# A state-space block and two attention layers on one core: token shift by transfers, packed step products, another set-up order, GpSimd's rotary work widened, the denominators' inverse on VectorE

## The reference, cut to what matters

```python
# state-space block, x: (16, 256, 128)
u = silu(causal_conv4(x @ in_w + in_b))
delta = softplus((u @ dt1_w + dt1_b) @ dt2_w + dt2_b)      # rank 16 between
h_t = exp(delta*A) * h_(t-1) + (exp(delta*A) - 1)/A * B * u     # 16 states per channel
y = (sum_n C_n h_n + D*u) * silu(x @ gate_w + gate_b)
x = layernorm(x + y @ out_w + out_b)
# twice:
h = shift_token(x)              # second 64 features come from the token before
q, k, v = split(h @ wqkv)       # 8 heads of 64
q, k = rotary_xpos(l2norm(q)*qs, l2norm(k)*ks)
x = x + local_attention(q, k, v, window 64, one window back) @ wo
h = layernorm(shift_token(x)) * g + b
a, g = split(h @ w1 + b1);  x = x + (a * gelu(g)) @ w2 + b2
# and a last residual and layernorm
```

## Time and profile before

| what | value |
|---|---|
| median of 3 runs | 1104.92 us (1102.85 to 1107.98) |
| the profiled execution's own time | 1106.03 us |
| its span in the profile | 1103.8 us |
| mean granted TensorE clock | 0.967 |
| instructions | 27452 |

### The profile page before, as it was taken

One profiled execution on the slowest core, in us unless ns is written; L12 is line 12 of the kernel. 1 busy time (PEld: TensorE's weight loads), 2 busy tenths in 40 slices (PEclk: granted clock), 3 DMA queues, 4 the chain that ended last, 5 costly groups with the idle time before them and its releaser, 6 DMA issues.

```text
span 1103.8 us, 27452 instructions
## 1 busy us (share of the span) xinstructions
PE 967.1 (88%) x10784; PEld 593.9 (54%) x10784; DVE 863.2 (78%) x1184; ACT 832.3 (75%) x1909; POOL 671.5 (61%) x513
## 2 busy tenths in 40 slices
PE   4677779799999899999999999998999999996775
PEld 1222345456555465557465646465665766665463
DVE  7776897898888877998799878996988875642543
ACT  4455777886998669886988699877879887783570
POOL 2004764688578666876567857685656777661561
PEclk9988899899999999999999999999999999998897
DMA  6000100000000100000000110010001011010010
GB/s 217 10 15 1 26 1 15 14 18 15 16 16 17 39 20 16 21 16 19 22 17 16 35 26 15 12 40 10 21 7 30 16 25 26 7 25 6 14 32 10
DMA packets 22354, 25.59 MB, mean 23 GB/s; under 512 B 2710, under 2 KB 14545, under 8 KB 22225
## 3 DMA queue, kind: packets, MB, share of 16 engines
q1 hardware_dynamic: 20783, 22.49, 7.9%
q10 hardware_dynamic: 1442, 1.34, 0.4%
HBM read 9.13 MB, written 2.10 MB: 10 GB/s over the span
## 4 chain that ended last, share of the span: by engine, by line
PE 47%; ACT 18%; issue 13%; DVE 11%; POOL 11%; ACTq 1%; POOLq 0%; DVEq 0%
PE M L1257 11%; PE YY L1257 10%; ACT prob L926 8%; PE AA L1257 8%; PE C L1257 6%; DVE scan L1073 4%; PE BB L1257 4%; POOL rn L761 4%; PE BB L1407 2%; PE BB L1395 2%; POOL rden L767 2%; PE C L1458 1%; ACT qkT L914 1%; ACT probT L895 1%; POOL kr L780 1%
## 5 line engine op out<-in xcount | busy, mean ns | idle before, releaser
L1073 DVE TENSOR_TENSOR_SCAN scan<-du,decay 128x1028 f32<-128x1028 f32 (+1 forms) x160 | 297.4, 1898 | 8.7 <-PE YY L1257 4.9
L926 ACT ACTIVATE prob<-BB,nbias,rn 128x128 f32<-128x128 f32 x472 | 208.7, 464 | 48.0 <-POOL nbias L774 47.3
L761 POOL TENSOR_TENSOR rn<-ssc,expo 128x16 f32<-128x16 f32 x64 | 212.5, 3321 | 19.8 <-ACT prob L926 15.1
L871 ACT ACTIVATE decay<-delta,negA 128x1024 f32<-128x1024 f32 (+1 forms) x160 | 153.3, 985 | 16.6 <-DVE scan L1073 12.1
L767 POOL TENSOR_TENSOR rden<-den,minus 128x8 f32<-128x8 f32 x64 | 126.5, 1976 | 49.5 <-ACT prob L926 49.5
L1257 PE MATMUL YY<-scan,diag 64*64 64x512 f32 (+1 forms) x1280 | 142.7, 538 | 15.3 <-DVE scan L1073 15.2
L1257 PE MATMUL AA<-wqkv,hT 128*128 128x512 f32 x256 | 131.4, 638 | 11.8 <-DVE qks L1148 10.2
L756 POOL TENSOR_SCALAR ssc<-ss 128x16 f32<-128x16 f32 x64 | 47.7, 745 | 91.1 <-DVE ss L1130 90.2
L1130 DVE TENSOR_REDUCE ss<-sq 128x16 f32<-128x1024 f32 x64 | 77.3, 1208 | 29.4 <-ACT sq L889 29.3
L926 ACT ACTIVATION_READ_ACCUMULATOR prob<-BB,nbias,rn 128x1 f32 x472 | 99.8, 211 | 0.0
L1162 DVE TENSOR_REDUCE nmax<-BB 128x8 f32<-128x1024 f32 x59 | 71.9, 1218 | 31.8 <-PE BB L1257 31.6
(11 more groups left out here) (158 smaller groups left out, 2062.4 us busy)
## 6 DMA issues: line engine op xcount, KB each, us to landing
v_even<-v_odd SPq DMA_DIRECT2D x96, 128.0 KB, 2.3
x<-in_x SPq DMA_DIRECT2D x6, 256.0 KB, 3.8
wqkv<-in_wqkv SPq DMA_DIRECT2D x1, 1536.0 KB
xT<-in_xT SPq DMA_DIRECT2D x6, 256.0 KB, 3.8
out<-outb SPq DMA_DIRECT2D x6, 256.0 KB, 2.6
w<-in_w SPq DMA_DIRECT2D x1, 682.0 KB
xT<-in_xT SPq DMA_DIRECT2D x4, 128.0 KB, 2.6
x<-in_x SPq DMA_DIRECT2D x4, 128.0 KB, 4.4
```

Of the source, the lines that this page charges most:

```text
L761: pool.tensor_tensor(rn[:, q % 2, :], ssc[:, :], expo[:, 0:2 * HEADS], ALU.pow).then_inc(rn_sb, 1)
L871: act.activation(decay[:, at % A_RING, both(g), 1:], delta[:, both(g), :], ACT.Exp, scale=negA[:, n:n + 1]).then_inc(decay_sb, 1)
L926: ins = act.activation(prob[:, h, :], bank_of(q, a)[:, c * P:(c + 1) * P], ACT.Exp, bias=nbias[:, q % 2, h:h + 1], scale=rn[:, q % 2, h:h ...
L1073: dve.tensor_tensor_scan(state, step, a, 0.0, ALU.add, ALU.mult).then_inc(scan_sb, 1)
```

## The change

- **Shift.** `shift` moves from PE to SP. Three transfers copy x2 to a new buffer `xs`: the second 64 features one partition down, the row that crosses a tile boundary, and the first 64 features unchanged. `ffn_stats`, `ffn_norm` and GpSimd's `residual` use `xs` or wait for the transfers. The shift and carry matrices are gone, and M is no longer held.
- **Step products.** dt1_w is padded to 32 columns. `rank` makes four products 128x32, one per channel half and half of the tokens, on four groups of 32 partitions of one bank; `step_in` makes four products 64x128, each over half the tokens and one half of the rows, and the sum over channel halves falls to that product. ScalarE reads each result in one instruction.
- **Set-up.** ScalarE issues two transfers, loads the exponential's table, makes A and loads silu's table; the others move to SP. GpSimd clears three buffers. VectorE computes the coefficients before the convolution. Masks and rotation tables become steps of the order, behind group 0's scans. In group 0, ScalarE makes the gate before u.
- **Rotary sums and norms.** `rotate` adds cosine and sine products for q and k together, in place, and multiplies both with their norms. `qk_T` transposes the result in 16 and not 24 transposes. Softmax needs no scale, its bias is the row maximum itself, and `exp_bias` is gone.
- **Inverse.** `inverse` moves from POOL's power to VectorE's `reciprocal`, a step of DVE's order that waits for the tile's softmax.
- The written orders of all engines are new.

```diff
-                pool.tensor_tensor(kr[:, :], qkc[:, q % 2, 1, :], qks[:, q % 2, 1, :], ALU.add).then_inc(rope_add, 1)
+                both_qk = qkc[:, q % 2].rearrange("p a x -> p (a x)")
+                pool.tensor_tensor(both_qk, both_qk, qks[:, q % 2].rearrange("p a x -> p (a x)"), ALU.add).then_inc(rope_add, 1)
...
+                pool.tensor_tensor(all_heads, all_heads, rn[:, q % 2, :].unsqueeze(2).to_broadcast((P, 2 * HEADS, DH)),
                                    ALU.mult).then_inc(qk_sb, 1)
...
-                pool.tensor_tensor(rden[:, q % 2, :], den[:, q % 2, :], minus[:, :], ALU.pow).then_inc(rden_sb, 1)
+            def inverse(q):
+                dve.wait_ge(prob_sb, 2 * q + 2)
+                if q >= 2:
+                    dve.wait_ge(o_sb, q - 1)
+                dve.reciprocal(rden[:, q % 2, :], den[:, q % 2, :]).then_inc(rden_sb, 1)
...
-                act.wait_ge(nmax_sb, q + 1)
+                act.wait_ge(max_sb, q + 1)
...
-                                             bias=nbias[:, q % 2, h:h + 1], scale=rn[:, q % 2, h:h + 1],
+                                             bias=nmax[:, q % 2, h:h + 1],
...
+            def shift(f):
+                n, mid = tiles_of(QUAD[f][1]), D // 2
+                sp.wait_ge(x2_sb, f + 1)
+                if f:
+                    sp.wait_ge(hn_sb, f)
+                else:
+                    sp.wait_ge(zeros_late, 1)
+                sp.dma_start(xs[1:P, 0:n, mid:], x2[0:P - 1, 0:n, mid:]).then_inc(sh_in, 16)
+                sp.dma_start(xs[0:1, 1:n:2, mid:], x2[P - 1:P, 0:n:2, mid:]).then_inc(sh_in, 16)
+                sp.dma_start(xs[:, 0:n, 0:mid], x2[:, 0:n, 0:mid]).then_inc(sh_in, 16)
...
-                pe.wait_ge(rope_mul, 2 * q + 2)
-                for part in range(2):
+                pe.wait_ge(qk_sb, q + 1)
+                for a in range(2):
                     for c in range(PAIRS):
                         for w in range(2):
...
+                            ins = pe.transpose(bank_of(q, w)[:, (a * PAIRS + c) * WIN:(a * PAIRS + c + 1) * WIN],
+                                               qkc[half(w), q % 2, a, c * P:(c + 1) * P], ident[half(w), half(w)])
...
-                for h in range(HALF):
-                    ins = mm(Y[0][0:RANK, 0:tok_of(g)], dt1_w[:, h, :], u[:, ab(g, h), 1:], h == 0, h == HALF - 1)
+                for k in range(2):
+                    for h in range(HALF):
+                        lo = (2 * k + h) * PART
...
+                        mm(Y[0][lo:lo + PART, 0:n], dt1_w[:, h, :], rhs).then_inc(d1_ps, 1)
...
-                    mm(bk(Y[h], g), dt2_w[:, h * P:(h + 1) * P], bk(dt1_s, g)).then_inc(z_ps, 1)
+                    for k in range(2):
+                        mm(Y[k][:, h * n:(h + 1) * n], dt2_w[half(k), h * P:(h + 1) * P], dt1_s[half(k), 0:n]).then_inc(z_ps, 1)
```

The set-up's code, in the same cut:

```diff
             load_xT(0)
+            sp.dma_start(pv[:, :], t["pv"]).then_inc(w_cols, 16)
             sp.dma_start(gate_w[:, :], t["gate_w"]).then_inc(w_gate, 16)
+            sp.dma_start(dt1_w[:, :, :], t["dt1_w"].rearrange("(h p) r -> p h r", h=HALF)).then_inc(w_step, 16)
+            sp.dma_start(dt2_w[:, :], t["dt2_w"]).then_inc(w_step, 16)
...
+            act.dma_start(in_w[:, :], t["in_w"]).then_inc(w_first, 16)
+            act.dma_start(bv[:, 0:NST], t["bv"][0:NST].partition_broadcast(P)).then_inc(w_rates, 16)
+            load_table(EXP_AND_LN)
+            act.wait_ge(w_rates, 16)
+            act.activation(negA[:, :], bv[:, BV["A_log"]:BV["A_log"] + NST], ACT.Exp).then_inc(a_exp, 1)
+            load_table(SILU)
...
+            coefficients()
+            dve.wait_ge(w_cols, 16)
             convolve(0, 0)
             convolve(0, 1)
-            coefficients()
-            masks()
-            rotation_tables()
+            state_weights()
```

More of the change, by code:

```diff
@@ L96 @@
[L96 to L125, removed]
@@ L171 @@
-shift 18, probs_T 62, weighted 62, norm_T 18, out_T 62, probs_T 63, up_gate 18, weighted 63, up_a 18 0,
-up_a 18 1, up_a 18 2, out_T 63, down 18, attn_out 19, shift 19, norm_T 19, up_gate 19, up_a 19 0, up_a 19 1,
-up_a 19 2, down 19"""
+state_y 1 14, state_y 1 15, mamba_out 1, u_in 2, gate_in 2, rank 2, qk_in 1, step_in 2, layer_T 0 1, qk_T 0,
+qk_in 2, scores 0, v_in 2, skip 2, qk_in 3, qk_T 1, state_y 2 0, probs_T 0, weighted 0, scores 1, out_T 0,
+v_in 3, state_y 2 1, state_y 2 2, probs_T 1, qk_T 2, scores 2, weighted 1, state_y 2 3, state_y 2 4, state_y 2 5,
@@ new lines @@
+norm_T 1, out_T 4, probs_T 5, v_in 7, qk_T 6, up_gate 1, state_y 3 2, scores 6, state_y 3 3, qk_in 8, up_a 1 0,
+state_y 3 4, weighted 5, up_a 1 1, state_y 3 5, probs_T 6, up_a 1 2, out_T 5, qk_in 9, v_in 8, qk_T 7,
+weighted 6, scores 7, state_y 3 6, state_y 3 7, out_T 6, state_y 3 8, down 1, probs_T 7, v_in 9, qk_T 8,
+weighted 7, state_y 3 9, scores 8, layer_T 1 1, out_T 7, qk_in 10, state_y 3 10, state_y 3 11, attn_out 2,
+probs_T 8, state_y 3 12, v_in 10, qk_T 9, state_y 3 13, scores 9, state_y 3 14, qk_in 11, state_y 3 15,
@@ new lines @@
+qk_in 16, up_a 3 1, qk_T 14, up_a 3 2, state_y 4 3, scores 14, down 3, out_T 12, attn_out 4, state_y 4 4,
+v_in 15, probs_T 14, weighted 13, state_y 4 5, state_y 4 6, out_T 13, qk_T 15, norm_T 4, v_in 16, up_gate 4,
+scores 15, up_a 4 0, qk_in 17, weighted 14, state_y 4 7, state_y 4 8, state_y 4 9, out_T 14, probs_T 15,
+up_a 4 1, v_in 17, qk_in 18, qk_T 16, weighted 15, up_a 4 2, scores 16, down 4, out_T 15, state_y 4 10,
+state_y 4 11, v_in 18, state_y 4 12, probs_T 16, state_y 4 13, qk_T 17, weighted 16, scores 17, state_y 4 14,
@@ L354 @@
-v_even 37, v_even 38, v_even 39, v_even 40, store 3, v_even 41, v_even 42, load_xT 8, load_x 8, v_even 43,
-v_even 44, v_even 45, load_xT 9, v_even 46, v_even 47, v_even 48, store 4, load_x 9, v_even 49, v_even 50,
-v_even 51, v_even 52, v_even 53, v_even 54, v_even 55, store 5, v_even 56, v_even 57, v_even 58, v_even 59,
-v_even 60, v_even 61, v_even 62, store 6, v_even 63, store 7, store 8, store 9"""
+conv0 1, conv1 1, mamba_norm 0, tables 0, masks 0, step_size 1, differences 1, scan 1 0, scan 1 1, scan 1 2,
@@ L360, in order @@
+v_even 63, shift 19, store 8, store 9"""
 def order(text):
@@ L1267, in free @@
                         pe.wait_ge(x2_sb, f + 1)
-                    elif last == "shift":
-                        pe.wait_ge(hn_sb, f + 1)
                     elif last == "norm_T":
```

642 lines of the change are left out of this document (315 added, 327 removed).

## The result

The changed kernel took 1178.07 us (median of 4 runs, 1172.85 to 1180.72) against 1104.45 us for the kernel before on the same chip: ratio 1.066, interval 1.061 to 1.070. It is 74 us slower, where the forecast had it 60 us faster, outside the range and beyond the rival on the slow side (1125).

The account below looks back on a forecast made before the run. TensorE, 95% busy from 250 to 950 us, was taken as the bound. From 1106.03 us, -6.5 - 5.5 - 3 - 48 + 0 + 3 = -60 gave 1046, forecast as 1045 us (range 1018 to 1082).

Parts of the forecast that it names:

- SP's part: Shift by SP transfers: statistics start 3.5 to 4.5 us after the sum, covered in the long stretch; uncovered, 30 us.
- the long stretch: 250 to 950 us, normalisation of 48 of 64 attention tiles: forecast 652 us instead of 700, 48 gained.
- TensorE sets the pace: From 250 to 950 us TensorE, busy 665.8 of 700 us (95%), was taken to bound the kernel.
- 111 us from TensorE: TensorE's whole loss of work by shift, transposes and step products, leaving it near 856 us busy in all.
- packed products: Step products on TensorE, 18.9 and 18.3 us for ten groups: 22 of the 37 us saved, 14 between 250 and 950.
- VectorE at 93%: In the long stretch VectorE becomes highest with 606 us of work at 93% busy, giving 652 us.
- Contention: VectorE's scans waiting for GpSimd's enlarged rotary sum and multiply: 6 us added, bounds 0 and 30.
- Rival 2: GpSimd and VectorE hold each other up, 30 us lost in the long stretch: total 1077 us, chance 0.13.
- TensorE's wait for the multiply at 0: Transposes behind GpSimd's multiply in the long stretch: cost put at 0, uncovered up to 2.5 us a tile.
- rival 5: Slower: TensorE waits uncovered at every tile's qk_T for GpSimd's multiply; at 2.2 us a tile 1125 us, chance 0.04.
- the start: Set-up and group 0: 6.5 us gained, first scan near 18 us and not 24.
- the reciprocal: VectorE gains 64 reciprocals of 128x8 at 200 ns, 12.8 us, 9.6 of it in the long stretch.

Follow-up runs that it names:

- the cut: Changed kernel with its first shift transfer (127 partitions) split into one of 112 and one of 15, nothing else: 1097.99 us, ratio 0.992.
- both losses out: Changed kernel with the split transfer, feed-forward reading an operand that needs no transfer wait, and GpSimd's multiply of q and k left out: 1059.93 us, ratio 0.960.

## Why the prediction was wrong

From the forecast of 1045 us to the measured 1178, in the steps that the runs separate: 1061 with neither the transfers' wait nor the multiply (16 over the forecast), +35 for these two (1096, measured 1098), +81 for the transfer over 127 partitions.

**SP's part failed first.** It priced three transfers from the v_even copy of 128 KB, which in the view above runs at about 200 GB/s, and took size for the measure. The count of partitions was the measure: 81 us. With the cut the latency was near its price, 4.9 us from sum to statistics in the quad above where 3.5 to 4.5 stood. But the prediction had "1.5 us x 20 = 30 us" if uncovered, and set it to 0 in the long stretch: measured 22 us, so mostly uncovered, even with the cut. Its other worry, v_even copies held behind the shift, came to one wait of 4.7 us on TensorE in the changed kernel. The Trainium skill names 127 partitions in the section cited above; weighed at this step, it would have given a rival of its own. By the 14 ns a piece measured here that is an estimated 7 us in a quad of four tiles.

**"TensorE sets the pace" was read from its busy share, and wrong.** The shift takes 62.0 us by its three groups. Taking it away lowered TensorE's total by 26.8 us (967.1 to 940.3) and the time by 2. Two errors lie in that. The matmuls of the groups run interleaved, and each group's busy time counts stretches that the others fill too, so groups must not be added. All 384 records that read x, the 64 layer transposes (11.8 us) among them, are busy 51 us together, where the groups add up to 74:

```profile
0.00:1103.80 1103.80, 50.95 (x384) 0.97 0.09 23
```

And a share of 95% in the earlier trace rows leaves 34 us of short waits in 700. Without the shift TensorE is busy 646.2 us of that stretch and no longer 665.8, at the same granted clock of 0.99, and idle for 54: the time given back turned into waits. A part of the small gain is the clock, too. From the first scan of group 8 to the end the kernel without the shift took 332 us and not 326, with a granted clock of 0.86 and not 0.92 after 950 us; from the first scan of group 2 to that of group 8 it was 4 us faster (661 against 665), at 0.98 in both.

The prediction took 111 us from TensorE and forecast 856 busy; the kernel without the multiply and the wait, its clock at 0.98 as good as before, has 893.1, a loss of 74. The packed products gave 20 of their 22, so shift and transposes together gave 54 where 89 stood; the transposes alone are not separated by any run at the same clock.

**VectorE at 93% was nearly reached, but not with the work forecast.** VectorE's total was sized well (880 us forecast, 888.6 measured with the cut), in part by terms that offset: the scans took 17 us more than their 6, the rest 9 less. From the first scan of group 2 to that of group 8, which holds the same 96 scans and 41 or 42 tiles in each kernel, the kernel before, the one with the cut transfer and the one with both losses out show (columns of the earlier trace rows):

```profile
112.50:777.70 665.20, 618.64 (x6958) 374.42 (x6958) 574.72 (x707) 548.67 (x1237) 462.94 (x321) 0.98 0.08 19
```

```profile
100.80:770.10 669.30, 591.07 (x6540) 347.67 (x6540) 606.22 (x754) 521.34 (x1238) 484.87 (x236) 0.97 0.10 23
```

```profile
99.10:739.70 640.60, 573.84 (x6540) 339.40 (x6540) 585.59 (x755) 520.76 (x1239) 374.21 (x194) 1.00 0.10 24
```

VectorE is busy 86%, 91% and 91%, TensorE 93%, 88% and 90%: VectorE did become the fuller engine. The forecast's terms, scaled to this stretch, are an estimated 588 us of VectorE (574.7 x 606 / 592) and 632 of span. With the cut it is 606 at 91%, 669: of the 37 us missing about 20 are work (up to 4 of them from one more tile in the stretch) and 17 the share. With both losses out it is 641, 9 over. That profiled execution was the fastest of its kernel's four (1052.1 us, median 1059.9), so this is its good side. The 93% itself was measured nowhere: it was set between VectorE's best 100 us and TensorE's share.

**Contention was 6, bounds 0 and 30.** The scans alone took 23 us more. The row on which it rested, one scan of 3309 ns, was the right one and was given too little weight; the longest scan now is 4.5 us (4.4 with the cut) and the longest multiply 3.9 with the cut. The long scans, kernel before and cut transfer:

```profile
L1073 DVE TENSOR_TENSOR_SCAN scan<-du,decay 128x1028 f32<-128x1028 f32 x96 | 222.1, 2346 | 3.1 <-PE YY L1257 2.5 <-ACT decay L871 0.5
```

```profile
L1075 DVE TENSOR_TENSOR_SCAN scan<-du,decay 128x1028 f32<-128x1028 f32 x96 | 243.2, 2564 | 4.9 <-PE YY L1263 4.5 <-ACT decay L872 0.4
```

The median of the long scans is 2285 ns in both. What all 160 take above the median of their length adds up to 7 us before, 31 with the cut and 17 without the multiply. The prediction's own argument, that chance and length of a meeting both double, makes 7 into 28, an addition of 21; it wrote 6 without this sum. That 21 is so near to 23 is partly luck: with the same rotary instructions in the old orders the scans took 309.1 us beside the pow and 322.1 without it, so it also depends on what happens to meet. The rule of the Trainium skill (Advanced Engine Details and Errata, VectorE Performance Modes), that GpSimd instructions and VectorE instructions in a two-port mode block each other, is borne out in its direction; that section does not name the scan. Rival 2 was real, at 15 us for the multiply alone.

**TensorE's wait for the multiply at 0** was nearly right in the new order (3.2 us in the row above), and rival 5, with 2.2 us a tile, was not what made the kernel slower. In orders that were not made for it the whole rotary part costs 57, with 39.0 us of TensorE's waits for the multiply at its transposes.

**Right were** the start (first scan at 17.86 us, "near 18" forecast), the packed products (37.2 us of groups down to 17.0 with the cut, 20 saved, 22 forecast), and the reciprocal (12.0 us at 187 ns, against 12.8 at 200). Softmax's wait for GpSimd, 51.0 us, went as forecast, but ScalarE now waits 46.7 us for the row maximum (63.0 without the cut), so little was gained by it. And of the start's 6.5 and the products' gains only 13 us reached the end in the kernel that has just these and the reciprocal. (GpSimd's share of the long stretch, "72%", is 71% by the prediction's own terms.)

What stays open: the worth of the rotary part in an order of its own against the old one in its own, since each order here fits one set of parts. Together, cut transfer and all, the changed kernel stands at 0.992 against 0.988 without shift and rotary parts, with intervals that touch, so with these orders the two parts bring nothing.

## What to carry to other kernels

Look at the partition count of a transfer before its size: 127 partitions went piece by piece, 14 ns each, and held the queue, and a cut at 112 or 120 gave 81 us for one more issue a quad. A high busy share is no proof that an engine sets the pace; leave its work out once and see (2 us here for groups that add up to 62), and don't add groups whose instructions interleave. With orders written by hand, swapping one part measures its misfit with the order; to price a wait, take away what it waits for and leave the order alone.

## What the runs showed of the hardware that was not expected

- A transfer between SBUF rows of 127 partitions ran at 13 to 19 GB/s, about 14 ns for a piece of 256 B, and the next issue on its queue took 6.4 us, though it moves 0.5 KB; with 112 or 120 partitions the next issue took 0.94 and 0.83 us.
- ScalarE's exponential of 128x128 with a row of bias alone takes 382 ns on the mean, where it took 464 with a scale per partition as well; in the kernel before with the rotary part alone it is 381:

```profile
L926 ACT ACTIVATE prob<-BB,nmax 128x128 f32<-128x128 f32 x472 | 165.7, 382 | 58.5 <-DVE nmax L1169 58.1
```

- TensorE's mean granted clock did not follow its busy share alone: from 250 to 950 us it was 0.94 in the changed kernel at 86% busy, 0.98 with the cut at 91%, and 1.00 without multiply and wait at the same 91%, against 0.99 at 95% in the earlier trace rows. What else it follows, no run here shows. The last of these kernels in that stretch, which reaches 100 us past its last scan:

```profile
250.00:950.00 700.00, 638.79 (x7484) 393.10 (x7484) 608.13 (x859) 567.40 (x1420) 408.40 (x231) 1.00 0.11 25
```
